# Slot map from one token code per tile and three bank pairs for the q/k units, in a fused attention and expert kernel

## What is computed

```python
# attention: 16 heads, each with two query/key halves of 8 values and a value of 16
a1, a2 = sdpa(q[..., 0], k[..., 0]), sdpa(q[..., 1], k[..., 1])
o = rms_norm(a1 - lam * a2, sub_norm_w) * (1 - LAMBDA_INIT)
attn = o @ w_proj.T + b_proj
# experts: 8 experts, capacity C = 1024 slots each, two choices per token
logits = tokens @ wg                     # 4096 x 8
idx1, idx2 = best, second best expert
loc1 = cumsum(mask1) - mask1             # place of a token in its expert
loc2 = cumsum(mask2) - mask2 + sum(mask1)
keep = loc < C
f = idx * C + min(loc, C - 1)            # slot
disp[f] += token * keep                  # 8192 slots
eo = gelu(disp @ w_gate) @ w_down
out = g1 * keep1 * eo[f1] + g2 * keep2 * eo[f2]
```

## Time and profile before

| | us |
|---|---|
| median of 3 runs | 1795.3 (1794.75 to 1795.95) |
| the profiled execution | 1794.24 |
| its span | 1792.4 |
| TensorE busy | 1713.7 (96%) |
| VectorE busy | 1481.2 (83%) |
| ScalarE busy | 1400.4 (78%) |
| GpSimd busy | 579.5 (32%) |

### The profile page before, as it was taken

The page is one execution under the profiler, slowest core; times in us unless marked ns, Lnnn a source line. Parts: engine busy times, 40 slices in busy tenths (PEclk is TensorE's granted clock), DMA queues, the critical chain, the costliest instruction groups (busy, mean ns, idle before and its releaser), DMA issues.

```text
span 1792.4 us, 39336 instructions
## 1 busy us (share of the span) xinstructions
PE 1713.7 (96%) x15554; PEld 747.2 (42%) x15555; DVE 1481.2 (83%) x1727; ACT 1400.4 (78%) x2639; POOL 579.5 (32%) x1065
## 2 busy tenths in 40 slices
PE   6868999999999999999999999999999999999998
PEld 5436888888885222222222222222222222222226
DVE  7766777777766999999999999999999999999913
ACT  4534454454444999999999999999999999999993
POOL 1475222221200223423243323423243323423261
PEclk9999999999999999999999999999999999999999
DMA  7655332122203111111111111111111111100003
GB/s 232 202 194 174 98 106 88 46 92 86 95 13 114 30 34 36 37 34 31 39 30 41 29 34 37 36 34 32 38 30 41 29 38 32 36 18 14 11 7 101
DMA packets 92280, 109.66 MB, mean 61 GB/s; under 512 B 17472, under 2 KB 67264, under 8 KB 92096
## 3 DMA queue, kind: packets, MB, share of 16 engines
q1 hardware_dynamic: 85952, 90.36, 16.1%
q0 software_dynamic: 6144, 16.79, 3.3%
HBM read 72.77 MB, written 33.82 MB: 59 GB/s over the span
## 4 chain that ended last, share of the span: by engine, by line
PE 66%; ACT 28%; POOL 3%; issue 1%; DVE 1%; DMA 1%; ACTq 0%; SPq 0%; DVEq 0%; POOLq 0%
ACT arena_t L781 25%; PE banks L1224 19%; PE banks L1212 11%; PE banks L1263 11%; PE banks L1243 10%; PE banks L1194 8%; POOL arena_v L558 2%; PE banks L1283 2%; ACT o_raw L760 2%; PE banks L1117 2%; PE banks L1345 1%; PE banks L1163 1%; PE banks L1128 0%; DMA arena_x<-x_in 0%; PE banks L1173 0%
## 5 line engine op out<-in xcount | busy, mean ns | idle before, releaser
L994 DVE TENSOR_REDUCE row_half<-banks 128x2 f32<-128x1024 f32 x1024 | 1187.4, 1217 | 133.7 <-PE banks L1194 129.3
L781 ACT ACTIVATE arena_t<-banks 128x512 f32<-128x512 f32 x2048 | 1083.4, 599 | 43.9 <-PE banks L1212 18.6
L1224 PE MATMUL banks<-arena_t,v_ring 128*17 128x256 f32 x8192 | 643.7, 386 | 25.4 <-ACT o_raw L760 25.3
L1224 PEld LDWEIGHTS banks<-arena_t,v_ring 128*17 128x17 f32 x8192 | 136.2, 95 | 408.7 <-issue 239.3
L1212 PE MATMUL banks<-arena_q 50*128 50x512 bf16 x960 | 284.0, 383 | 0.0
L1212 PE MATMUL banks<-qk_ring 50*128 50x512 bf16 x896 | 264.6, 386 | 5.6 <-ACT arena_t L781 2.9
L1194 PE MATMUL banks<-arena_q 48*128 48x512 bf16 x960 | 269.7, 384 | 0.2 <-DVE row_half L994 0.2
L1194 PE MATMUL banks<-qk_ring 48*128 48x512 bf16 x896 | 250.2, 382 | 0.9 <-DVEq L987 0.9
L745 ACT ACTIVATE arena_t<-banks 128x512 f32<-128x512 f32 x128 | 76.5, 598 | 205.9 <-PE banks L1243 197.2
L1263 PE MATMUL banks<-w_parts,hidden_parts 128*128 128x256 f32 x1536 | 196.3, 286 | 0.0
L1263 PEld LDWEIGHTS banks<-w_parts,hidden_parts 128*128 128x128 f32 x1536 | 187.1, 192 | 13.4 <-issue 13.4
(11 more groups left out here) (146 smaller groups left out, 1352.4 us busy)
## 6 DMA issues: line engine op xcount, KB each, us to landing
expert_rows<-arena_r SPq DMA_DIRECT2D x16, 512.0 KB, 3.0
q_stack<-arena_q SPq DMA_DIRECT2D x8, 768.0 KB, 5.5
k_stack<-arena_q SPq DMA_DIRECT2D x8, 768.0 KB, 3.5
v_heads<-arena_v SPq DMA_DIRECT2D x4, 1088.0 KB, 5.6
v_ring<-v_heads SPq DMA_DIRECT2D x64, 68.0 KB, 2.8
arena_x<-x_in SPq DMA_DIRECT2D x4, 1024.0 KB, 6.3
token_rows<-arena_x SPq DMA_DIRECT2D x4, 1024.0 KB, 7.8
arena_v<-w_gate_in SPq DMA_DIRECT2D x4, 1024.0 KB, 6.3
```

Source lines behind the costliest of these rows:

```text
L781: nc.scalar.activation(probs[:, kt % PSLOTS, q, :], banks[:, ST_BANKS[ring_place(i) % 3], :], ACT.Exp).then_inc(exp_done, 1)
L994: nc.vector.tensor_reduce(halves[:, :, j // 2], banks[:, SMAX_PAIRS[m % 2]:SMAX_PAIRS[m % 2] + 2, :], AX.X, ALU.max, negate=True).then_inc ...
L1224: mm = pe.matmul(banks[QUAD * q:QUAD * q + VP, OT_BANK, columns], v_ring[:, g % SLOTS, kt, :], probs[:, kt % PSLOTS, q, columns], start=(k ...
```

## The change

- Both sides of the map are laid out by slot place or slot tile first and by pair k = (choice, token tile) last. A new table `numbers` (128 x 64 bf16, row n holds n, made once by a GpSimd iota, in the first half of arena_v) is compared with the bf16 slot parts: four operations of 32 rows for low_side, two for tile_side, then two products with `token_code`. All on DVE, one per unit from unit 2 to unit 9.
- `token_code` is one bf16 number per pair, (128 + lane) x 2^(token tile), made by GpSimd with five doublings. One product replaces first token and lane; the sum in PSUM is decoded from its bits (find_tokens).
- The map runs behind unit 10, its 64 matmuls have 64 columns in place of 128, and read both operands at a step of 64 elements. find_tokens comes at the end of unit 10 instead of in unit 12.
- q/k units use three bank pairs, so unit n waits for unit n - 3; the first rows are transposed into banks 6 and 7.
- The gate load moves behind unit 7's plane loads and waits for four of the side operations. ScalarE makes both high parts (behind units 10 and 13), DVE both low parts (at unit 10 and after unit 15).
- ScalarE loads the Gelu table after the Exp calls of unit 0 and the Exp table after the last expert step. The middle and low parts of unit 15 move into expert step 0, behind f = 1; TensorE waits there for unit 15's rest.

```diff
-COUNT_AT, MAP_AT, ROWS_AT = 1, 11, 14
+COUNT_AT, MAP_AT, ROWS_AT = 1, 10, 14
+SIDES = 8
+HIGH_AT = (10, 13)
+FIRST_CODE = 134 * 2 ** 7
...
+        numbers = arena_v[:, 0:2 * W_PART].bitcast(BF16).rearrange("p (n k) -> p n k", n=P)
+        low_side = arena_v[:, 2 * W_PART:4 * W_PART].bitcast(BF16).rearrange("p (n k) -> p n k", n=P)
+        tile_side = arena_r[:, 4 * CH:8 * CH].bitcast(BF16).rearrange("p (n k) -> p n k", n=TILES)
...
-        FIRST_ROWS_BANK, ROWS_BANK = 4, 2
+        FIRST_ROWS_BANK, ROWS_BANK = 6, 2
...
+        def qk_bank(n):
+            return 2 * ((n + 1) % 3)
...
-            load_gate(0, 0)
...
+                    if n == 7:
+                        sp.wait_ge(sides_ready, 4)
+                        load_gate(0, 0)
...
+            nc.gpsimd.iota(numbers, pattern=[[1, P], [0, 2 * NT]], base=0, channel_multiplier=0,
...
+            for k in range(5):
+                pool.wait_ge(code_step, k + 1)
+                nc.gpsimd.tensor_scalar(token_code[:, :, 2 ** k:2 ** (k + 1)], token_code[:, :, 0:2 ** k], 2.0 ** 2 ** k, None,
...
-            for i in range(LOW_BY_POOL):
-                c, t = divmod(i, NT)
-                low = nc.gpsimd.tensor_scalar(low_side[:, c, t, :], in_tile[:], slot_low[:, c, t:t + 1], None, ALU.is_equal)
-            low.then_inc(low_side_ready, 1)
-            first_weights_low(0)
             pool.wait_ge(xn_out, 16 * B)
             pool.wait_ge(map_ready, 1)
             for n in range(2):
                 find_rows(n)
-            pool.wait_ge(down_in[0], 16)
-            nc.gpsimd.tensor_copy(w_parts[0][:, 1, HI], w_ring[0][:, 1, LO]).then_inc(first_high, 1)
-            first_weights_low(1)
...
             for n in range(4 * B):
+                part1(n)
                 if n == ROWS_AT:
                     rows_t_high(0)
+                if n + 1 < 4 * B:
+                    middle(n)
                 if n == 0:
...
+                    load_table(ACT.Gelu)
+                if n == HIGH_AT[0]:
+                    act.wait_ge(sides_ready, 6)
+                    first_weights_high(0, gate_in)
+                if n == HIGH_AT[1]:
+                    first_weights_high(1, down_in)
...
+                    if n == 0 and f == 1:
+                        middle(4 * B - 1)
...
+            load_table(ACT.Exp)
...
+            def over(ap, rows):
+                return ap[:].rearrange("p c t -> p (c t)").unsqueeze(1).broadcast_to([P, rows, 2 * NT])
+
+            HALF_S, QUARTER = TILES // 2, P // 4
+
+            def tile_is(h):
+                rows = slice(h * HALF_S, (h + 1) * HALF_S)
+                nc.vector.tensor_tensor(tile_side[:, rows, :], numbers[:, rows.start + 1:rows.stop + 1, :], over(tile_bf, HALF_S),
+                                        ALU.is_equal).then_inc(sides_ready, 1)
...
+            def low_is(q):
+                rows = slice(q * QUARTER, (q + 1) * QUARTER)
+                nc.vector.tensor_tensor(low_side[:, rows, :], numbers[:, rows, :], over(low_bf, QUARTER),
+                                        ALU.is_equal).then_inc(sides_ready, 1)
...
             for n in range(4 * B):
                 split_rest(n)
                 if n == COUNT_AT:
                     find_slots()
...
+                if n in (COUNT_AT + 1, COUNT_AT + 2):
+                    low_is(n - COUNT_AT - 1)
+                if n in (COUNT_AT + 3, COUNT_AT + 4):
+                    tile_is(n - COUNT_AT - 3)
+                if n in (COUNT_AT + 5, COUNT_AT + 6):
+                    low_is(n - COUNT_AT - 3)
+                if n in (COUNT_AT + 7, COUNT_AT + 8):
+                    tile_tokens(n - COUNT_AT - 7)
                 if n == ROWS_AT:
                     rows_t_low(0)
-                split_low(n)
+                if n + 1 < 4 * B:
+                    split_low(n)
+                if n == MAP_AT:
+                    first_weights_low(0)
+                    find_tokens()
+            first_weights_low(1)
...
+                pe.wait_ge(sides_ready, SIDES)
+                for k in range(2 * NT):
+                    mm = pe.matmul(banks[:, MAP_BANK, 0:TILES], low_side[:, :, k], tile_side[:, :, k],
+                                   start=(k == 0), stop=(k == 2 * NT - 1))
...
-                if n >= 2:
-                    pe.wait_ge(rest_ready, n - 1)
+                if n == 1:
+                    pe.wait_ge(v_copied, NT)
+                if n >= 3:
+                    pe.wait_ge(rest_ready, n - 2)
...
+                    if n == 0 and f == 1:
+                        pe.wait_ge(rest_ready, 4 * B)
```

More of the change, by code:

```diff
@@ L713, in rows_t_high, with part1 @@
                     nc.scalar.copy(rows_parts[:, HI, c, :], banks[:, rows_bank(n) + c, :]).then_inc(rows_high, 1)
-            for n in range(4 * B):
+            def part1(n):
                 s = n % PARTS
```

119 lines of the change are left out of this document (40 added, 79 removed).

## The result

The changed kernel takes 1799.39 us (median of 20 runs, 1794.26 to 1801.29), the kernel before, beside it on the same chip, 1794.76 (20 runs, 1793.15 to 1796.38). The medians are 4.6 us apart; the ratio of all runs (means 1798.80 and 1794.73) is 1.0023, with a 95% interval from 1.0016 to 1.0029: 4.1 us longer, where the forecast had 3.1 us less. The profiled execution's span is 1798.3 us (1792.4 before), and R, the point at which the forecast stops to count, is at 167.44 us; forecast 162.3, before 165.41.

The account below looks back on a forecast made before the run. Bound by SyncE's issue queue up to the down load, then by TensorE's steady pattern. Landing 135.2 plus 27.1 gave R 162.3 against 165.41, 3.1 us less: 1792.2 from the median 1795.3; range 1788.5 to 1797.5.

Parts of the forecast that it names:

- R: TensorE's first row maximum after the third down block of expert step 0; forecast 162.3 us against 165.41 before.
- (a): GpSimd's 40 comparisons, down weights copy and low parts (4.51 us each) go; no direct gain, but the map runs early.
- (b): VectorE's side work becomes eight 2048-element operations in units 2 to 9, taken at 1.2 us each, ends 0.98 and 2.28.
- (e): Gate weights' high copy behind unit 10; token numbers at about 117, 8 to 9 us earlier, rows by 129.5, off the path.
- rival 2: Side operations run at 2.28 us, unit 4's store 3.0 later, R 165.3, total 1795.2, no change; chance 0.13.
- (c): Gelu table load ahead of unit 1's first part costs 1.4 us; unit 4's low part ends at 83.65 against 83.06.
- Rival 4: At the front, the number table's 8192-element GpSimd iota could hold VectorE's layer-norm work, at most 1 us; no chance given.
- (d): SyncE's store queue sends the down load at 128.2, 1.0 us later than before; its wait for the map costs nothing.
- Rival 3: Stepped operands slow the map's matmuls; at four times the price 23.7 us, R 169.1, total 1799; chance 0.08.
- (f): ScalarE's down weights copy behind unit 13 waits for the down load, taken to land in 7.0 us, at 135.2.
- (g): From the down load's landing: experts start 5.5 us later, unit 15's store 15.0, expert 1's gate load 23.4, R 27.1.
- (h): No gain counted for the Gelu load gone from the experts' start (1.28 us) or the Exp load before attention.

Follow-up runs that it names:

- the combined kernels: Changed kernel with GpSimd's fills late, no early Gelu load, and the down weights split in the expert step, behind unit 14, or that plus earlier down load: ratios 0.9983, 0.9982, 0.9977.

## Why the prediction was wrong

- **(a), (b), (e): right.** Side operations 1.21 to 1.22 us (1.2 taken). So rival 2 is out. Map at 105.21 (104.9), token numbers at 117.88 (about 117). The Trainium skill (VectorE: DVE Perf Modes, the perf-mode tier table) gives 1224 ns for such an operation, and the trace agrees.
- **(c): right in kind, and short by the front.** The table load was charged at 1.4 and cost 1.5. But unit 4's store came at 84.90, not 83.65, because unit 0 started 1.5 us later. Rival 4 named the place with "at most 1 us" and the iota as the cause; it was the fills that the iota pushed back, and the prediction's sum has nothing for them. The first part of the failure: 1.25 us.
- **(d): right in its sum, by two errors that cancel.** From unit 4's store to the down load 44.46 us (44.52 forecast). But the queue's own pace was 4.9 us, not 5.3, and unit 11's store waited for unit 11 behind the longer map, 8.5 us behind unit 10's. That the two came out even is luck. "Its wait for the map costs nothing" failed: with half of the map's matmuls the load goes out 2.7 us earlier. Rival 3's slack failed too. It gave the map about 15 us before anything is lost, 5.5 more than the 9.5 that it takes; then 10.2 of the 15.7 us added ahead of it, and 7.3 of the 12.8, should have arrived at R − u0, and 12.0 and 10.3 did. What the real lengthening (5.9 to 9.5) costs in R is not shown: with the half map the load lands no earlier. A version with both sides of the map in a row was not run. Rival 3's ground was right (a step costs TensorE a factor, 149 against 54 ns at the same clock, 1.6 times the old map's 92), its size of four times not. The Trainium skill (SBUF — State Buffer, the note on cachelines in the section on the DMA port swizzle) says that each access that crosses to a new 16-byte line pays a penalty. These runs agree in direction; the number is theirs.
- **(f): the step that failed most.** The mechanism is as forecast and was the cause: with the copy one unit later the kernel is level with before. The term was mis-sized: the load took 9.6 us, not 7.0, so L was 139.0 instead of 135.2, of which 1.2 is the later issue and 2.6 the landing. In the second profile of the changed kernel it took 8.9. The reason for 7.0 doesn't carry it. The gathers were nearly over, as forecast: the last was issued at 129.47, just behind the load, and their queue moved 0.30 MB during its flight, against 0.41 in before. The flight was as long as before's 9.2 all the same, with the load and two stores of 768 KB filling the DMA engines (share 0.76 to 1.06 from 130 to 139 us). Which of these sets the length was not tested, but the rate hardly differs: 2.88 MB moved during this flight (300 GB/s), 2.62 in before's (281), 3.54 and 3.70 in the two flights of 12.0 and 11.9 us with more gathers beside them (295 and 311). Where the map was lengthened and the gathers were over (0.01 MB), only 1.58 MB moved and the load landed in 6.7 us; 7.0 belongs to such a stretch. The only row of a down load at this place had 9.2, and it should have been taken. The forecast's own upper end, 9.2, gives L = 137.4.
- **(g): right but for one load.** Experts at L + 5.5 (5.5 forecast), expert 1's gate load out at L + 18.7 (18.5). It landed in 5.9, not 4.9: its copy starts at L + 24.7 instead of 23.4, R is at L + 28.4 instead of 27.1.
- **(h): right.** In the combined kernels, which have the table load back at the first Gelu, it costs nothing there.
- **The sum.** 1.2 at the issue, 2.6 in the landing and 1.3 behind it make the 5.1 us by which R missed. The times differ by 4.1 us from before, R by 2.5 in the mean of the profiles. The remaining 1.6 lie behind R, where VectorE's gap (2.0 us, in one profile of two, so 1.0 on average) and a tail of 40.9 against 39.8 on average would make 2.1. Both vary between executions of one kernel. Whether the changed kernel draws them more often stays open; two profiles can't tell.
- **The range.** It took the late landing as an end (R 164.5 for 9.2) but never together with a late front and a second slow load. All three delays add, since they lie one behind the other on the same path; bounds on one path should have been added, not compared.

## What to carry to other kernels

A load's flight time belongs to what else the DMA engines carry in that stretch: take it from the row at that place, not from a middle with a quicker one elsewhere. When a wait for a load is put into an in-order engine's program, look at what stands behind it; here one unit's difference in place, with the same load landing at the same time, was worth 4.3 us. A GpSimd job moved or enlarged at the start must be laid beside VectorE's timeline, and a table load belongs where its engine waits anyway.

## What the runs showed of the hardware

- TensorE with bf16 operands at a step of 128 bytes: about 149 ns a pair of 128 stationary and 64 moving columns, at granted clocks of 0.50 and 0.82 to 1.00 alike, against 54 ns in a row at 0.50. Moving columns pay about 1 ns each, stationary ones about 0.25.
- GpSimd's fills (16-bit, 1024 elements, four in 3.63 us) hold some of VectorE's operations until the end of a fill: 1.99 us instead of 0.17 for 8 elements, 3.44 instead of 0.23 for a conversion of 128, both to the end of the last of the four, and 1.05 to the end of the third in the run with the late copy; the statistics and their aggregation (0.64 at 13.65, as in before) were not held. A bf16 iota of 8192 elements (7.59 us, 0.93 ns each) does the same: an operation that began 0.15 to 0.43 us before its end finished 0.08 behind it.
- A 1 MB load issued at about 129.5, when the gathers were nearly all out, took 9.6 and 8.9 us in the changed kernel's two profiles. Issued at 125.6 and 119.8, with 0.73 and 1.01 MB of gathers beside it, it took 12.0 and 11.9. The DMA engines moved 281 to 311 GB/s during each of these flights and before's. Issued at 144.8, with the gathers over, it took 6.7.
- The output stage of one unchanged kernel took 38.4, 40.1 or 41.8 us, by whether the granted clock was at 0.50 for about 3 us behind TensorE's waits at no place, one or two.
